# Two-layer transformer kernel on one core: maxima and down matmuls placed into the seams between stages, and four exponent banks for the end of the last two groups

## The reference

```python
# layer 0 attention: 16 heads of 16, causal
dots = einsum('bhid,bhjd->bhij', q, k) * d ** -0.5
attn = softmax(where(causal, -inf, dots))
x = layernorm(x + (attn @ v) @ w_out + b_out)
# layer 0 feed-forward, weights made ternary: 256 -> 1024 -> 256
x = layernorm(x + (silu(x @ Wu.T) * (x @ Wg.T)) @ Wd.T)
# layer 1 attention: 16 query heads, 4 key/value heads, q from x * sigmoid(sum|x|)
qk = q k / sqrt(16) - slope_h * |i - j|;  qk = where(inside_window_or_global, -1e9, qk)
x = layernorm(x + (softmax(qk) @ v) @ Wo + bo)
# layer 1 feed-forward, fp32 weights: silu(x @ w_gate.T) * (x @ w_up.T), then w_down
```

## Time and profile before

| | |
|---|---|
| median of three runs | 1057.06 us (1056.75 to 1057.12) |
| the profiled execution | 1056.31 us, span 1054.6 us, mean granted clock 0.975 |
| PE, PEld busy | 977.1 us (93%), 517.4 us (49%) |
| DVE busy | 695.1 us (66%) |
| ACT busy | 598.9 us (57%) |
| POOL busy | 347.9 us (33%) |
| exponents, ACT line 1089 | 896 instructions, 436.0 us |
| maxima, DVE line 1024 | 256 of layer 0 and 256 of layer 1, 754 and about 1155 ns each |
| values, PE line 1161 | 1792 matmuls, 211.4 us |

### The profile page before, as it was taken

How to read it: one execution, slowest core, us unless ns; L and a number is a source line. 1 busy time by engine, 2 the same in 40 slices (tenths; PEclk the granted TensorE clock), 3 DMA queues, 4 the chain that set the end, 5 groups by cost and what they waited for, 6 DMA issues and landing times. The chain is left out here.

```text
span 1054.6 us, 18023 instructions
## 1 busy us (share of the span) xinstructions
PE 977.1 (93%) x6546; PEld 517.4 (49%) x6546; DVE 695.1 (66%) x1535; ACT 598.9 (57%) x1204; POOL 347.9 (33%) x418
## 2 busy tenths in 40 slices
PE   6798999999987999988799999999999989899997
PEld 4443333333334788664324343333434344698896
DVE  2877878878824666579787888788877824225323
ACT  4445777777765434345367767777777767323221
POOL 3031312221112445232335363533425252324323
PEclk9898999999998999998899999999999999999999
DMA  7552211122000200043614050312211000000001
GB/s 253 169 180 88 62 48 34 43 61 61 2 2 6 85 1 1 23 147 94 165 54 161 9 170 1 129 51 80 94 38 38 1 2 1 1 1 21 21 1 40
DMA packets 32996, 64.20 MB, mean 61 GB/s; under 512 B 6095, under 2 KB 22367, under 8 KB 30532
## 3 DMA queue, kind: packets, MB, share of 16 engines
q1 hardware_dynamic: 31564, 58.47, 17.9%
q0 software_dynamic: 1072, 3.80, 1.1%
q10 hardware_dynamic: 272, 0.79, 0.2%
HBM read 50.45 MB, written 12.32 MB: 60 GB/s over the span
## 5 line engine op out<-in xcount | busy, mean ns | idle before, releaser
L1089 ACT ACTIVATE prob<-ps 128x512 f32<-128x512 f32 (+6 forms) x896 | 436.0, 536 | 189.0 <-PE ps L1132 181.1
L1132 PE MATMUL ps<-qop,kop 98*128 98x512 bf16 (+14 forms) x1376 | 281.7, 290 | 12.7 <-DMA qop<-mrow 6.1
L1118 PE MATMUL ps<-kop,qop 96*128 96x512 bf16 (+3 forms) x896 | 229.5, 357 | 17.5 <-DVE maxes L1024 10.2
L1132 PEld LDWEIGHTS ps<-qop,kop 107*128 107x128 bf16 (+1 forms) x1376 | 105.5, 97 | 260.5 <-ACT prob L1089 215.1
L1161 PE MATMUL ps<-prob,vst 128*32 128x512 f32 (+4 forms) x1792 | 211.4, 544 | 7.5 <-POOL prob L955 3.3
L1024 DVE CUSTOM_DVE_ANT_0 sums<-ps,tri 128x128 bf16<-128x128 f32 (+7 forms) x256 | 181.0, 754 | 32.0 <-PE ps L1118 27.9
L961 POOL TENSOR_TENSOR prob<-prob,keep 128x384 int32<-128x384 int32 (+2 forms) x144 | 122.7, 853 | 208.7 <-ACT prob L1089 207.4
L1024 DVE CUSTOM_DVE_ANT_0 sums<-ps,table 128x960 bf16<-128x960 f32 x128 | 148.1, 1157 | 62.5 <-PE ps L1118 48.9
L1558 PE MATMUL ps<-xs,wffn 128*128 128x512 f32 x640 | 156.2, 400 | 3.7 <-PEq L799 2.2
L1024 DVE CUSTOM_DVE_ANT_0 tri<-ps,table 128x960 bf16<-128x960 f32 x128 | 147.5, 1152 | 2.9 <-PE ps L1118 2.9
L1456 POOL TENSOR_TENSOR hs<-hf,hs 128x512 fp32r<-128x512 f32 x64 | 82.9, 1297 | 161.2 <-ACT hs L1483 161.1
(11 more groups left out here) (103 smaller groups left out, 686.9 us busy)
## 6 DMA issues: line engine op xcount, KB each, us to landing
table<-in_table SPq DMA_DIRECT2D x32, 464.0 KB, 4.6
qop<-q_parts SPq DMA_DIRECT2D x96, 128.0 KB, 2.6
kop<-k_parts SPq DMA_DIRECT2D x48, 128.0 KB, 2.6
kop<-k_parts SPq DMA_DIRECT2D x48, 96.0 KB
q_parts<-qop SPq DMA_DIRECT2D x8, 384.0 KB, 3.4
q_parts<-kop SPq DMA_DIRECT2D x8, 384.0 KB, 2.6
x<-in_x SPq DMA_DIRECT2D x4, 512.0 KB, 5.7
k_parts<-qop SPq DMA_DIRECT2D x4, 384.0 KB, 2.7
```

Source lines behind the costliest of these rows:

```text
L1089: nc.scalar.activation(prob[0:rows, q % 2, k % HG, lo % CH:lo % CH + hi - lo], ps[0:rows, t_bank(n, k), lo % CH:lo % CH + hi - lo], ACT.Ex ...
L1118: last = nc.tensor.matmul(ps[:, S_BANK + score_slot(L, k)[0] + a // CH, a % CH:a % CH + b - a], qop[0:RD, par, h, i0:i0 + P], kop[0:RD, pa ...
L1132: return nc.tensor.matmul(ps[:, bank, a % CH:a % CH + b - a], lhs, rhs, start=start, stop=True, skip_group_check=True)
```

## The change

Six edits. (1) At the end of each opening, behind "parts" and "rows" of group 0, the first 6 (layer 0) or 4 (layer 1) max units of group 1 are placed (`AHEAD`); group 0's own list starts its maxima behind them, and the first string of `GIVEN` is written anew (36 instead of 42 maxima), with two numbers of `VALUES_BEHIND`. (2) In the opening of layer 1 the first three down steps come before the first maximum. (3) Exp steps use four banks from exp step 36 of group 6 in layer 0 (its last three quads) and step 56 of group 6 in layer 1 (its last two), with `exp_before` as the rule for which exponent must be done. (4) In group 7 of layer 0 every values step stands behind all four exp steps of the next quad, as in layer 1. (5) Between chunks of the feed-forward, the next chunk's first unit comes before the downs, its second one between down steps 2 and 3, and every down is split: blocks 0 to 5 of all four, then 6 and 7. (6) The plans' start of the stream of maxima follows `AHEAD`. No computation is added or removed; PE has the same matmuls, ACT, DVE and POOL the same instructions, and SP's and POOL's order is unchanged.

```diff
+AHEAD = (6, 4)
-GIVEN = ("3111 0110 2210 0200 1111 2011 1022 1100 2000 2210 0200 1002",
+GIVEN = ("1101 1210 0200 0110 0220 1101 2020 2001 1010 2110 0200 0102",
          "0210 1100 0210 0200 1102 0010 2110 0011 0100 3110 0200 1002")
-VALUES_BEHIND = ((4, 4, 4, 3, 3, 2, 3, 3, 4, 4, 3), (3, 4, 3, 3, 2, 4, 2, 3, 4, 4, 3))
+VALUES_BEHIND = ((4, 4, 4, 2, 3, 2, 3, 2, 4, 4, 3), (3, 4, 3, 3, 2, 4, 2, 3, 4, 4, 3))
...
-    values_behind = VALUES_BEHIND[late]
-    stream = [("max", k, 1) for k in range(lead if late else 0, nu)] if group + 1 < N else []
+    values_behind = (HG,) * (nq - 1) if last else VALUES_BEHIND[late]
+    stream = [("max", k, 1) for k in range(lead if late else AHEAD[0], nu)] if group + 1 < N else []
...
-    work, given, at = sum(share for _, _, share in behind), 0.0, 0
+    at = 3 if layer.index == 1 else 0
+    out += [(what, k, 0) for what, k, _ in behind[:at]]
+    work, given = sum(share for _, _, share in behind[at:]), 0.0
...
-    return out + [("parts", 0, 1), ("rows", 0, 1)]
+    return out + [("parts", 0, 1), ("rows", 0, 1)] + [("max", k, 2) for k in range(AHEAD[layer.index])]
...
+    FREE = (N - 2) * NX + HG * (NQ - KEY_TILES_AHEAD[i] + 1)
...
         def t_bank(n, k):
-            return exp_slots(n)[k % len(exp_slots(n))]
+            banks = T_BANKS if n * NX + k < FREE else LAST_T_BANKS
+            return banks[k % len(banks)]
+        def exp_before(n, k):
+            j = n * NX + k
+            back = 2 if j < FREE + 2 else 4
+            if j < 2 or FREE + 2 <= j < FREE + 4:
+                return None
+            return j - back
...
-                        if n == N - 1 and k == len(T_BANKS):
+                        if n * NX + k == FREE + len(T_BANKS):
                             pe.wait_ge(max_done, N * NU)
-                        if k >= slots or (n >= 1 and k < len(T_BANKS)):
-                            pe.wait_ge(exp_done, n * NX + k + 1 - (slots if k >= slots else len(T_BANKS)))
+                        if exp_before(n, k) is not None:
+                            pe.wait_ge(exp_done, exp_before(n, k) + 1)
...
-            for u in range(c * KE + 2, min((c + 1) * KE + 2, NC * KE)):
+            for u in range(c * KE + 2, (c + 1) * KE):
                 self.unit(pe, u)
             if c < NC - 1:
+                self.unit(pe, (c + 1) * KE)
                 for j in range(CT):
-                    self.down(pe, c, j, 0, KE)
+                    if j == CT // 2:
+                        self.unit(pe, (c + 1) * KE + 1)
+                    self.down(pe, c, j, 0, KE - 2)
+                for j in range(CT):
+                    self.down(pe, c, j, KE - 2, KE)
```

More of the change, by code:

```diff
@@ L147, in plan @@
     lead = nu * KEY_TILES_AHEAD[layer.index] // nq
-    stream = [(k, 1) for k in range(lead if group >= 1 else 0, nu)] if group + 1 < N else []
+    stream = [(k, 1) for k in range(lead if group >= 1 else AHEAD[1], nu)] if group + 1 < N else []
     stream_next = [(k, 2) for k in range(lead)] if group + 2 < N else []
@@ L807, in attend @@
         opening = opening_of(L, proj)
-        def exp_slots(n):
-            return LAST_T_BANKS if n == N - 1 else T_BANKS
         def t_bank(n, k):
-            return exp_slots(n)[k % len(exp_slots(n))]
+            banks = T_BANKS if n * NX + k < FREE else LAST_T_BANKS
[6 more added lines that the diff above has]
+            return j - back
         def all_groups(step):
@@ L1202, in step @@
                             pe.wait_ge(v_staged, (n + 1) * (1 + i))
-                        slots = len(exp_slots(n))
-                        if n == N - 1 and k == len(T_BANKS):
+                        if n * NX + k == FREE + len(T_BANKS):
                             pe.wait_ge(max_done, N * NU)
-                        if k >= slots or (n >= 1 and k < len(T_BANKS)):
-                            pe.wait_ge(exp_done, n * NX + k + 1 - (slots if k >= slots else len(T_BANKS)))
+                        if exp_before(n, k) is not None:
+                            pe.wait_ge(exp_done, exp_before(n, k) + 1)
                         shifted(k, b, t_bank(n, k)).then_inc(t_full, 1)
```

## The result

The change takes 1048.05 us (median; 1046.86 to 1049.61), the kernel before, on the same chip, 1057.09 us (1056.75 to 1057.26). The ratio is 0.9912, 95% interval 0.99 to 0.9923: 9.0 us faster where 14.4 were forecast, near the upper end of the range. The profiled execution took 1047.74 us, its span is 1046.0 us, its mean granted clock 0.975, the same as before.

What follows compares the result with a forecast made beforehand. PE, busy 93% of the span, was taken as the bound, with its idle and half-clock time in seams to win. Terms 2.2 + 3.3 + 1.7 + 1.8 + 4.4 + 1.0 = 14.4 us gave 1042.7 us, range 1037 to 1049.5.

Steps and rivals of the forecast that it cites:

- its own case: The forecast's case, in which the summed terms hold: 1042.7 us, range 1038 to 1047, chance 0.67.
- rival 1: The moved maxima give nothing back: A, C and D are 0, 7.2 us are left, 1049.9 us; chance 0.2.
- the last two groups: Layer 0's groups 6 and 7: exponent-bank, mask and last-exponent waits shrink, −4.4 us; layer 1's group 6, −1.0 us.
- the chunk seams: Between feed-forward chunks: layer 0's PE waits of 1.08 and 0.70 us both go, −1.8 us; nothing in layer 1.
- D: Layer 1, opening to group 0: four early maxima fill PE's wait, clock returns sooner; −3.3 us (−1 to −5.5).
- A: Layer 0, opening to group 0: six early maxima fill PE's wait, clock returns sooner; −2.2 us (0 to −5).
- C: First feed-forward to layer 1's opening: three down steps first fill PE's wait, clock never falls; −1.7 us (+0.6 to −4).
- rival 3: Groups 0: PE works at DVE's pace with holes, clock stays low, kernel slower, up to 1080 us; chance 0.02.
- Rival 2: DVE bounds both groups 0: A and D give its whole idle time and the clock; 21.6 us, 1035.5; chance 0.09.

Runs made afterwards that it cites:

- the fillers: Kernel before, nothing moved, plus 512-column matmuls whose result nobody reads, in PE's idle stretches at both openings' ends and in layer 0's group 7: 1053.92 us, ratio 0.9971.
- A alone: Kernel before with only the six early maxima in layer 0's opening and the first string of the table: 1057.35 us, ratio 0.9999; a second trace took 1057.09 us.
- the change without C: The changed kernel with the down steps of layer 1's opening between the maxima again, as before: 1047.28 us, ratio 0.9904 to the kernel before.
- C alone: Kernel before with only three down steps put ahead of layer 1's first maximum: 1058.68 us, ratio 1.0004 (0.9989 to 1.002).
- the change without A: The changed kernel without the early maxima of layer 0, with the old first string: 1047.81 us, ratio 0.9898 to the kernel before.

## Why the prediction was right and wrong

**The number.** 1048.05 us lies outside the range that the prediction gave for its own case, 1038 to 1047; it lies inside the stated one, to 1049.5, because that took in most of rival 1, whose 1049.9 is nearer to it than the forecast's 1042.7. The terms of the last two groups and of the chunk seams held, D's in part, A's and C's gave nothing in the total. That the time fell inside the range is thus owed to the rival and not to the sum.

**What A is worth.** T0 to T1 of layer 0 in all fourteen traces, by the length of the low clock there:

| low clock | without A | with A |
|---|---|---|
| 13.7 us | | 31.36, 30.85 |
| 10.2 us | 30.86, 30.86, 30.99 | 30.12, 29.84, 30.02 |
| 6.8 us | 30.24, 30.38, 30.32 | |
| none | 29.14, 29.15 | 27.90 |

Read across, six early maxima are worth 0.9 us at the same length of low clock (30.90 less 29.99) and 1.25 at full clock. The placing was priced at 1.3 less 0.2 for the later exponent, so as a whole that step held within 0.2 us. Its parts held less well. At half clock the first exponent is not later at all (3.24 to 3.30 us behind T0 with A, 3.25 to 3.40 without). And "half clock explains half of 5.6 us, 2.8" was too much: the fillers show 1.66, which leaves 2.4 of the 4.1 us for the ten extra maxima, 0.24 each and not 0.13. The pair at full clock, one trace each, has 1.94 for six, 0.32 each. DVE's idle time, 3.6, was too much by all of these.

Read down, the length of the low clock moves the same stretch by up to 1.8 us without A and 3.5 with it. So the step that failed is "As for the clock, PE is at work again 3 us earlier, so the full clock should be back up to 3 us earlier": it was back later. Counted from T0, the clock is full again after 6.8 to 9.2 us in the six traces without A and without fillers, and after 10.4 to 13.7 in the five with A. The length depends on when the clock falls as well. Where it fell 1.0 to 1.3 us before T0, the low stretch was 10.2 us long without A (three traces) and 13.7 with it (one); where it fell at T0 or up to 0.7 us behind, it was 6.8 us long without A (three) and 10.2 (three) or 13.7 (one) with it. So the early maxima lengthened it wherever the two can be compared, as rival 3 had it. That takes back most of what the placing gives: as the traces came, T0 to T1 is 30.6 us in the mean without A and 30.4 with it, which fits a total that shows nothing.

Both traces of A alone also have 1.6 us more at the beginning of the second feed-forward, where the kernel before has none. That it is A which brings that stretch is not shown: the four early maxima alone, the change without C and the fillers alone have it too, the change itself has it in neither trace.

**D.** T0 to T1 of layer 1, in the same way: with 10.2 us of low clock 51.05 to 51.17 us without D (four traces) and 48.61 to 49.02 with it (three); with 6.8 us 50.70 and 50.74 against 48.03 and 48.27; at full clock 49.95 against 47.66. D is worth 2.3 to 2.6 us at each, where the placing was priced at 2.6 less 0.4. From first exponent to transpose 3.15 us went in the change's trace and 3.05 at full clock, 0.76 a maximum where 0.65 was taken. "0.4 lost" measured 1.05, and at full clock still 0.76 (3.30 to 4.06 us behind T0), so only 0.3 of it is the half clock; most of the rest is DVE's 1.16 us for each maximum. The clock's 1.1 did not come: its low stretch has the same two lengths with D as without. That is most of what is missing of the 3.3.

**C.** "But the clock never falls" is the sentence that failed. It doesn't fall at the first maximum, but at the projection behind a row of waits for DVE, 3.4 us long, in all four traces with C, and in two of them, C alone and the change without A, 13.7 us later once more. The kernel before had a second low stretch, too (479.0, for 6.8 us), which the prediction left out. And "what that is worth is read on DVE, which is nearly full" took 88% for a bound: the other 12% contains waits for ACT's rounding of k and q. The early gain was 0.15 us in DVE's first two waits, not 1.45 less 0.6, and the longer waits for ACT, 1.05 us more at k alone, outweigh it. That these waits grew because the clock was low at the projection fits all four traces; a run with C and a full clock there was not made. −1.7 us was forecast, c_only's interval is −1.2 to +2.1; the change without C is, if anything, faster. Rival 1 ("it gives nothing back") was right for C and for A in the total, wrong for D.

**Chunk seams, last groups.** Every term of these held: 1.8 forecast, 1.7 measured; 4.4 forecast, 4.36 in the trace (3.5 in the second one, where the low clock at the end was 10.2 us long instead of 6.8); 1.0 forecast, 1.1. Compared at the same low clock, T7 to F of layer 0 is 4.2 us shorter each time: at 10.2 us 49.28 to 45.09 (means of five and of four traces), at 6.8 us 48.59 to 44.38, without one 48.04 to 43.88. Each of these terms was a wait on one engine with the instruction that releases it beside it, and the order of the new release known. How the 4.4 divide into group 6, group 7 and the last exponent was not tried.

**Rival 3**, the clock that stays low, had a chance of 2 in 100 as something that outweighs the gain. In small it is what happened to A: not a loss in the total, but a low clock that ends later and takes back most of the placing. In D the clock's term of 1.1 us came to nothing without a longer low stretch. Of the difference between the forecast and the change's first trace, 5.8 us, 2.7 are A, 1.2 D, 0.7 C and the chunk seams together, and 1.3 the opening, which scatters (T0 stood between 80.62 and 82.31 us over the fourteen traces). **Rival 2** (DVE is the bound) falls as it was priced: at full clock A gives 1.25 us and D 2.3 (1.94 and 3.05 from the first exponent on), not 3.6 and 4.4. The upper ends that the prediction took from the caution of the Trainium skill ("Perfetto Trace Analysis", Identifying the Most-Contended Engine), that matmul busy time says little and that occupancy is a fair measure for the other engines, were further off than the price from two stretches of the trace, 0.8 and 2.6.

The Trainium skill ("TensorE: Matmul & The Clock Gate", HAM oscillation) describes a loop whose short bursts of matmuls, with waits for DMA between them, keep falling back to the low clock. The runs with fillers agree in kind: work of no use in the seams kept the clock full there and is worth 3.1 us on the kernel before and 6.3 on the change without C. The same page of the Trainium skill (Part 1) also holds that the number of slow matmuls at the start varies from run to run and isn't to be fitted. The traces agree on the variation; on this kernel the low clock is not small beside an edit, 1.7 us at one seam.

## What to carry to other kernels

A wait that is filled with thin work does not yet bring the full clock. Take the gain of the placing and that of the clock as two terms, and give the second nothing until a trace shows it: here PE rests 2 us ahead of the transpose, too, which no edit of the change touched, and the clock fell there. The fillers stood before that rest as well as behind it; which of them kept the clock up was not tried apart. Price a moved piece of work by comparing two stretches of the same trace that differ in its count, but do not take the clock's share in them for half of the low stretch: here it was 2.8 and 2.5 by that rule and 1.7 and 1.05 in the traces. When an edit takes a wait away, look whether the engine waits longer just before, as DVE did in C. And where a seam stays at the low clock, try matmuls that nobody reads: they cost little where PE waits anyway, and gave more here than A and C.

## What the runs showed of the hardware

- The same order of instructions gets low stretches of different length from one execution to the next: at T0 of layer 0 6.8 or 10.2 us in traces without A, 10.2 or 13.7 with it, the longer one of each pair mostly where the clock fell before T0, and the length alone moves the stretch by 0.6 us (30.9 to 30.3) or 1 us (31.1 to 30.0). A difference of one microsecond between two traces of one execution each is no verdict on an edit.
- Half clock cost far less than half of its length at these seams: 10.2 us of it cost 1.7 us at T0 of layer 0 (30.86 to 29.14) and 1.1 at T0 of layer 1 (51.05 to 49.95).
- A full clock at one seam is no promise for the next. The 3.4 us at the start of the second feed-forward cost 1.6 us and came in five of fourteen traces, among kernels that differ only hundreds of microseconds earlier. What decides it stays open.
- Fillers gave 3.1 us on the old order and 6.3 on the new one. In the traces of the new order without and with them (spans 1047.9 and 1038.4 us, further apart than the medians) 3.0 us lie in layer 0's group 0, 1.0 at the end of group 7, 2.5 from the first feed-forward to layer 1's T0, 0.6 in layer 1's group 0 (30.85, 44.92, 169.24, 48.27 against 27.90, 43.88, 166.74, 47.66) and 1.6 at that scattering stretch of the second feed-forward.
